# Scores of the small attention: GpSimd's share of the products moved to VectorE, two products and one wide sum per token block

## What is computed

```python
qkv = jnp.einsum('bnm,fm->bnf', x, Wqkv).reshape(b, n, 16, 24)
q, k, v = qkv[..., :8], qkv[..., 8:16], qkv[..., 16:]
scores = jnp.einsum('bnhd,bngd->bnhg', q, k) / 8.0
attn = jax.nn.softmax(scores, axis=-1)
out = jnp.einsum('bnhg,bngd->bnhd', attn, v)
```

## Time and profile before

| | |
|---|---|
| median of three runs | 1473.27 us |
| the profiled execution | 1472.66 us, span 1470.9 us, mean granted TensorE clock 0.986 |
| TensorE (PE) busy | 1395.0 us, 95% |
| VectorE (DVE) busy | 942.5 us, 64% |
| ScalarE (ACT) busy | 865.2 us, 59% |
| GpSimd (POOL) busy | 515.5 us, 35% |
| the chain that ended last | PE 68%, issue 12%, DVE 10%, POOL 4%, ACT 3% |

### The profile page before, as it was taken

How to read it: one execution, slowest core, us unless ns; L and a number is a source line. 1 busy time by engine, 2 the same in 40 slices (tenths; PEclk the granted TensorE clock), 3 DMA queues, 4 the chain that set the end, 5 groups by cost and what they waited for, 6 DMA issues and landing times.

```text
span 1470.9 us, 34497 instructions
## 1 busy us (share of the span) xinstructions
PE 1395.0 (95%) x12096; PEld 1237.2 (84%) x12096; DVE 942.5 (64%) x2534; ACT 865.2 (59%) x2361; POOL 515.5 (35%) x415
## 2 busy tenths in 40 slices
PE   5897999999999999999999999999999999999837
PEld 4685989898898989989898898989889898988737
DVE  4456575775766667576666757677575667757482
ACT  4565756656575565657656565765757566574303
POOL 2307052350705325070532607043260704416140
PEclk9899999999999999999999999999999999999978
DMA  7000000000000000000000000000000000000000
GB/s 255 5 2 5 1 2 8 0 7 0 0 7 0 7 0 7 0 0 7 0 7 0 7 1 0 7 0 7 0 1 6 0 7 0 4 2 1 5 4 4
DMA packets 14089, 13.78 MB, mean 9 GB/s; under 512 B 1626, under 2 KB 12771, under 8 KB 13795
## 3 DMA queue, kind: packets, MB, share of 16 engines
q1 hardware_dynamic: 14050, 13.27, 2.8%
HBM read 11.17 MB, written 2.10 MB: 9 GB/s over the span
## 4 chain that ended last, share of the span: by engine, by line
PE 68%; issue 12%; DVE 10%; POOL 4%; ACT 3%; POOLq 2%; DVEq 1%; DMA 0%; SPq 0%; ACTq 0%
PE bank_F L1100 16%; PE bank_S L982 5%; PE bank_T L1011 4%; PE bank_A L1039 4%; PE bank_A L1024 3%; PE bank_T L968 3%; DVE hid L742 3%; PE bank_T L969 3%; PE bank_T L970 3%; PE bank_A L1032 3%; PE bank_A L969 3%; PE bank_A L968 3%; PE bank_A L970 3%; PE bank_F L968 2%; DVE neg_max L651 2%
## 5 line engine op out<-in xcount | busy, mean ns | idle before, releaser
L1100 PE MATMUL bank_F<-down,hid 128*128 128x128 f32 x3072 | 373.5, 277 | 16.3 <-DVE x L730 15.6
L1100 PEld LDWEIGHTS bank_F<-down,hid 128*128 128x128 f32 x3072 | 357.9, 192 | 25.5 <-DVE x L730 16.6
L543 ACT ACTIVATE probs<-bank_S,neg_max 128x256 f32<-128x256 f32 x512 | 236.0, 475 | 168.1 <-DVE neg_max L651 168.1
L651 DVE TENSOR_REDUCE neg_max<-bank_S 128x2 f32<-128x512 f32 x256 | 164.6, 684 | 72.8 <-PE bank_S L982 69.8
L471 POOL TENSOR_TENSOR hid<-hid,qkv 128x1024 f32<-128x1024 f32 x62 | 177.0, 2867 | 39.8 <-ACT hid L559 39.8
L730 DVE SCALAR_TENSOR_TENSOR x<-bank_F,gates,x 128x128 f32<-128x128 f32 x512 | 154.9, 344 | 47.8 <-PE bank_F L1100 37.6
L522 ACT ACTIVATE probsT<-bank_T 128x512 f32<-128x512 f32 x256 | 139.6, 605 | 47.0 <-PE bank_T L1011 46.9
L441 POOL TENSOR_TENSOR mean_sq<-sum_sq,one_over_d 128x2 f32<-128x2 f32 x16 | 3.2, 197 | 448.6 <-ACT h_row L517 448.6
L1011 PE MATMUL bank_T<-ident,probs 128*128 128x128 f32 x1024 | 138.2, 278 | 0.2 <-ACT probs L543 0.2
L459 POOL TENSOR_TENSOR hid<-qkv 128x1024 f32<-128x1024 f32 x47 | 112.2, 2388 | 66.7 <-ACT qkv L522 66.7
L1011 PEld LDWEIGHTS bank_T<-ident,probs 128*128 128x128 f32 x1024 | 112.2, 141 | 25.5 <-issue 21.3
(11 more groups left out here) (167 smaller groups left out, 3194.7 us busy)
## 6 DMA issues: line engine op xcount, KB each, us to landing
x_row<-in_x SPq DMA_DIRECT2D x16, 128.0 KB, 2.1
down<-in_w SPq DMA_DIRECT2D x1, 2048.0 KB, 15.2
out<-x SPq DMA_DIRECT2D x16, 128.0 KB, 1.8
hid<-in_w SPq DMA_DIRECT2D x1, 1536.0 KB, 7.8
hid<-in_rw SPq DMA_DIRECT2D x1, 1024.0 KB, 7.4
hid<-in_wv SPq DMA_DIRECT2D x1, 512.0 KB, 3.8
hid<-in_wq SPq DMA_DIRECT2D x1, 512.0 KB, 4.7
hid<-in_wk SPq DMA_DIRECT2D x1, 512.0 KB, 5.5
```

The lines of the kernel that those rows point to most:

```text
L543: ins = sc.activation(probs[:, h // 2 % 2, h % 2, t, :], unit.bank(f"S{h}")[:, t * S:(t + 1) * S], ACT.Exp, bias=neg_max[:, h, t:t + 1], a ...
L651: ve.tensor_reduce(neg_max[:, h, :], v.bank(f"S{h}")[:, :].rearrange("p (t k) -> p t k", t=NT), AX.X, ALU.max, negate=True).then_inc(max_r ...
L1100: ins = te.matmul(bank[:, (j * NT + t) * P:(j * NT + t + 1) * P], hid[:, e, k, tokens(t)], down[:, e, k, :], start=k == 0, stop=k == m - 1)
```

## The change

VectorE makes all four half products and sums them over the whole 8 numbers, both halves of a block in one instruction of 2048 elements. For t = 0 the two products are at step 4 and the sum with the shift at step 5, for t = 1 at steps 6 and 7. GpSimd's `head_product` and the semaphore `prod_ready` go; `value_product` stays on GpSimd.

```diff
@@ gpsimd @@
-            def head_product(v):
-                for t, i in ((0, 1), (1, 0), (1, 1))[0 if v.a else 1:]:
-                    if (t, i) != (1, 1):
-                        pool.wait_ge(*v.drain(f"LQ{t}"))
-                    q, k = head_pairs(t, half(i))
-                    settled(pool, g.tensor_tensor(prod[:, t, half(i)], q, k, ALU.mult))
-                    ins = add_pairs(prod[:, t, half(i)], DH1)
-                    if i == 1:
-                        ins.then_inc(prod_ready, 1)
...
-                    head_product(v)
                     if v.a:
                         value_product(v, 0)
                     value_product(v, 1)
@@ vector @@
-            def head_product(v):
-                dve.wait_ge(*v.drain("LQ0"))
-                for i in range(1 if v.a else 2):
-                    q, k = head_pairs(0, half(i))
-                    ins = ve.tensor_tensor(prod[:, 0, half(i)], q, k, ALU.mult)
-                    if i == 1:
-                        ins.then_inc(prod_ready, 1)
-                    settled(dve, ins)
+            def head_product(v, t):
+                dve.wait_ge(*v.drain(f"LQ{t}"))
+                for i in range(2):
+                    q, k = head_pairs(t, half(i))
+                    ins = ve.tensor_tensor(prod[:, t, half(i)], q, k, ALU.mult)
+                settled(dve, ins)
...
-            def head_sum(v, t, i):
-                if (t, i) != (0, 0):
-                    dve.wait_ge(prod_ready, v.at(1, NT, t + 1))
-                own = t == 0 and (i == 0 or not v.a)
-                n = DH1 if own else DH1 // 2
-                settled(dve, ve.reduce_sum(score1[:, t, half(i)], prod[:, t, half(i), :, 0:n], AX.X))
+            def head_sum(v, t):
+                settled(dve, ve.reduce_sum(score1[:, t].rearrange("p h g -> p (h g)"), prod[:, t].rearrange("p h g d -> p (h g) d"), AX.X))
...
-                    if v.b and s == 4:
-                        head_product(v)
-                    if v.b and s in (5, 6):
-                        head_sum(v, s - 5, 0)
-                        head_sum(v, s - 5, 1)
-                        head_shift(v, s - 5)
+                    if v.b and s in (4, 6):
+                        head_product(v, s // 2 - 2)
+                    if v.b and s in (5, 7):
+                        head_sum(v, s // 2 - 2)
+                        head_shift(v, s // 2 - 2)
```

More of the change, by code:

```diff
@@ L310, in transformer_blocks @@
         exp1_ready = sem("exp1_ready")
-        prod_ready = sem("prod_ready")
         pv1_ready = sem("pv1_ready")
```

## The result

The changed kernel takes 1567.84 us (median of four runs, 1566.21 to 1571.04); the kernel before, in the same comparison, 1474.08 us. The ratio is 1.0635, with a 95% interval from 1.0611 to 1.066: slower by 6.4%. The forecast was 1565 us.

A forecast was written before the change was run, and what follows sets the result against it. TensorE bounds the loop, busy 86.01 of 86.30 us per iteration. 15 x (5.4 us delay + 0.7 clock) + 1 for iteration 16 = 92.5 us on 1472.66 gives 1565 us; range 1528 to 1588.

The forecast's parts named there:

- Step 4: VectorE's two products of block 0 in a row: about 2.4 us, the next instruction starting 0.94 us earlier.
- Step 5: VectorE's wide sum of block 0: 2.3 us, 0.25 lost with the drain; everything behind it still 0.68 us earlier.
- Step 6: VectorE's two products of block 1 take turns with GpSimd's instructions, each waiting out the other's: from 735.04 to 740.4.
- a shared port: VectorE and GpSimd only slow each other at block 1's products: done 0.8 us earlier, some 12 us less over the run.
- Step 7: Block 1's wide sum ahead of `o_scale` of O7, which ends at 747.45 against 741.87; TensorE waits 3.3 us within OUT.
- GpSimd's chain and X1T: Block 1's value products on GpSimd delay `inverse_std` of x1: X1T 5.2 us late, 5.4 us per iteration in all.
- the sign named for this step: TensorE idle before X1T, the wait ended by line 695, which waits for GpSimd.
- The clock: TensorE's clock halves after the wait in OUT, two iterations in three: 0.7 us per iteration, ends 0 and 1.7.
- the one without a collision: Block 1's products take 2.5 us, engines' turns falling otherwise: 30 to 35 us in all, 1505; chance 0.15, including partly hidden delay.
- Its variant: At block 1, VectorE's first product blocked, its second ahead of GpSimd's addition: 1.2 us less per iteration, 1547 us.
- The rival that the added work fits into idle time: VectorE's idle time takes the added work, GpSimd's slow instructions go, TensorE gains 0.29 us: 1468 us, chance 0.03.

## Why the prediction was right

The time (1565 forecast, 1567.84 measured) and most of its terms hold. Times below count from the first product of step 4.

- **Step 4** was to end 0.94 earlier, with two products in 2.4: it is 0.90 (2.51 to the next instruction instead of 3.41) and 2.36.
- **Step 5**: wide sum 2.3 forecast, 2.29 measured; lead at step 6 0.68 forecast, 0.67 measured (15.02 against 15.69).
- **Step 6**: 5.3 forecast for the two products, 5.22 measured, with the turns in the order that was worked out: VectorE after GpSimd's product, GpSimd's addition next, VectorE last. The exclusive lock of the Trainium skill ("SBUF — State Buffer", section "Who interferes with whom") agrees with GpSimd's addition of 2.06 for 1.26; a shared port would have given 4.5 or so.
- **Step 7**: `o_scale` of O7 5.58 late in the forecast, 5.49 in the trace (26.91 against 21.42); waits of 1.4 and 3.3 forecast before and within OUT, 1.39 and 3.21 measured.
- **GpSimd's chain and X1T.** The forecast had X1T 5.2 late at full clock, held by `inverse_std` behind the value products. The one iteration of the loop without a fall of the clock has its first product at 211.26 and these rows (timelines of VectorE and TensorE, changed kernel):

```profile
243.12 0.60 DVE L681 TENSOR_SCALAR x<-x,mv,std_inv 128x128 f32<-128x128 f32 x2 [0.41 <-POOL std_inv L426]
...
243.30 0.39 PE L949 MATMUL bank_A<-wv_hi,hT_hi 128*128 128x512 f32 x1
243.78 0.44 PE L931 MATMUL bank_A<-ident,x 128*128 128x128 f32 x2
```

  X1T is 32.52 after the product, 4.9 late. VectorE does wait for GpSimd, but only 0.41 us; V0's last matmul (243.30 + 0.39) ends just before. GpSimd's chain and TensorE's own queue arrive together, so the sign named for this step, TensorE idle before X1T, did not come, and the term was 0.3 too large.
- **The clock** was the term with the widest bounds, 0 to 1.7 us per iteration with 0.7 taken. In the iteration shown first a fall costs 33.65 - 32.52 = 1.13 us (1.05 forecast), but falls come nearly every time, not two times in three. Windows of the changed kernel over stretches of 92 us:

```profile
191.00:283.00 92.00, 87.23 (x762) 77.11 (x762) 63.76 (x161) 53.91 (x150) 20.64 (x19) 1.00 0.02 4
...
835.00:927.00 92.00, 87.41 (x758) 77.86 (x756) 63.24 (x159) 53.15 (x148) 20.58 (x19) 0.98 0.01 3
```

  Of the 13 stretches from 191 to 1387 us, only this first one has 1.00. Here the rule of the Trainium skill ("TensorE: Matmul & The Clock Gate", Part 1: idling halves the clock), taken as a fall behind every such wait, was nearer than my two in three, though the first stretch had its wait of 3.21 us and no fall. The two errors, 0.3 too much and 0.4 too little, nearly cancel: the mechanism was right, but that the time came within 3 us is partly luck.

Of the rivals, the one without a collision was priced at 1505 us. The run that takes the collision away (1546 us) does so by making GpSimd wait, which costs AOT 1.9 us and leaves the clock's falls in, so that price stays untested as it stood. Its variant, in which VectorE's second product comes ahead of GpSimd's addition, is ruled out by the trace: the addition took its turn first. The rival that the added work fits into idle time fails at the point named for it: `o_scale` of O7 is needed 23.0 us after the first product and comes at 27.3.

## What to carry to other kernels

Before work is moved between VectorE and GpSimd, look at what the other engine does at the moment when it would run: VectorE's products of two SBUF tensors and GpSimd's products and additions took turns here, whole instruction by whole instruction, and a product of 1.2 us cost 1.3 to 3.3 us depending only on its place in the queue; sums over one tensor did not wait. Read the price of a moved step not from the engine's busy share but from the nearest instruction behind it that the bounding engine waits for, here `o_scale` of O7, with 1.2 us of slack. And when a wait of 2 to 3 us is opened in TensorE's stream, add the clock to the bill: here it came to 14 of the 94 us.

## What the runs showed that was not expected

- `ln_apply` of x1, which reads one tensor and two numbers per partition, waits for GpSimd as the products do: 5.17 us instead of 0.60 beside two value products. I had put that only on instructions that read two tensors.
- More work in TensorE's loop can cost more than its own time: with 20 more matmuls per iteration the packets of instruction DMA went from 24 to 133, and TensorE waited about 1.0 us at the loop's start; with 5 more (25 packets) it did not. That the instructions were fetched anew in each iteration is my reading of these counts; no run shows it directly.
- The clock fell in a run whose steady waits in the loop were 2.06 and 1.87 us (mean granted clock 0.968), while a wait of 2.89 us in the kernel before was followed by 1.00.
